# An attention layer's row maxima: which units use a difference, and where the fourth maximum stands in TensorE's queue

## The reference

```python
q = (hidden_states @ wq).reshape(B, S, H, D)      # B, S, H, D = 4, 1024, 16, 16
k = (hidden_states @ wk).reshape(B, S, Hkv, D)    # Hkv = 4
v = (hidden_states @ wv).reshape(B, S, Hkv, D)
...
scores = jnp.einsum('bqkgd,bskd->bkgqs', qg, k) * scale
attn = jax.nn.softmax(scores, axis=-1)
out = jnp.einsum('bkgqs,bskd->bqkgd', attn, v).reshape(B, S, E)
...
x = _layernorm(x + _L0_attn_ref(...), axis=-1)
x = _layernorm(x + _L0_ffn_ref(...), axis=-1)
```

## Time and profile before

| | us |
|---|---|
| median of 3 runs | 1069.21 |
| lowest, highest | 1068.98, 1076.9 |
| the profiled execution | 1073.24 |
| its span, first to last instruction | 1071.2 |

### The profile page before, as it was taken

The page is one execution under the profiler, slowest core; times in us unless marked ns, Lnnn a source line. Parts: engine busy times, 40 slices in busy tenths (PEclk is TensorE's granted clock), DMA queues, the critical chain, the costliest instruction groups (busy, mean ns, idle before and its releaser), DMA issues.

```text
span 1071.2 us, 16022 instructions
## 1 busy us (share of the span) xinstructions
PE 988.0 (92%) x5632; PEld 485.4 (45%) x5632; DVE 807.5 (75%) x1601; ACT 710.3 (66%) x908; POOL 237.4 (22%) x162
## 2 busy tenths in 40 slices
PE   7886999999999999999999999999998899999985
PEld 3443433333333333333333333333333778778774
DVE  2756688888788888888788888888862677777756
ACT  1224588888888888888888888888885433333332
POOL 9854563000000000000000000000000444444443
PEclk9885599999999999999999999999999999999997
DMA  5659532032132331322304213131110201111001
GB/s 164 222 172 187 127 103 64 26 75 78 32 65 57 69 63 44 71 55 50 78 22 79 73 39 64 52 72 42 29 49 12 61 0 41 40 40 40 20 20 40
DMA packets 48450, 70.65 MB, mean 66 GB/s; under 512 B 15152, under 2 KB 27184, under 8 KB 48368
## 3 DMA queue, kind: packets, MB, share of 16 engines
q1 hardware_dynamic: 47552, 66.45, 24.6%
q0 software_dynamic: 816, 3.15, 0.9%
HBM read 46.47 MB, written 16.25 MB: 59 GB/s over the span
## 4 chain that ended last, share of the span: by engine, by line
PE 59%; DVE 21%; issue 5%; POOL 4%; ACT 4%; POOLq 0%; DVEq 0%; ACTq 0%
PE ring_bank L948 25%; PE pv_bank L971 23%; DVE block_max L607 15%; PE pair_bank L1068 6%; POOL hid_l L528 2%; PE pv_bank L1077 2%; PE pair_bank L1021 1%; ACT probs L867 1%; DVE hid L758 1%; PE ring_bank L1077 1%; DVE x L675 1%; POOL rstd L513 1%; PE ring_bank L987 1%; ACT hid_h L883 1%; ACT silu L893 1%
## 5 line engine op out<-in xcount | busy, mean ns | idle before, releaser
L867 ACT ACTIVATE probs<-pair_bank 128x1024 f32<-128x1024 f32 x512 | 496.7, 1028 | 54.3 <-PE pair_bank L1021 54.3
L607 DVE TENSOR_REDUCE block_max<-ring_bank 128x1 f32<-128x512 f32 x660 | 421.8, 685 | 114.5 <-PE ring_bank L948 111.4
L948 PE MATMUL ring_bank<-k_max,q_sb 64*128 64x512 f32 x1024 | 365.1, 492 | 37.1 <-DVE block_max L607 9.8
L948 PEld LDWEIGHTS ring_bank<-k_max,q_sb 64*128 64x128 f32 x1024 | 148.0, 191 | 365.3 <-DVE block_max L607 224.3
L971 PE MATMUL pv_bank<-probs,v_sb 128*32 128x512 f32 x2048 | 274.5, 608 | 1.4 <-ACT probs L867 1.3
L1021 PE MATMUL pair_bank<-q_sb,k_sb 64*128 64x512 f32 x1024 | 230.9, 403 | 1.9 <-ACT probs L867 1.9
L838 ACT ACTIVATE above<-ring_bank 128x512 f32<-128x512 f32 x182 | 109.4, 603 | 73.7 <-PE ring_bank L948 70.7
L509 POOL TENSOR_TENSOR attn<-attn,inv_rows 128x1024 f32<-128x1024 f32 x8 | 19.5, 2434 | 590.3 <-DMA inv_rows<-inv_d 590.3
L1021 PEld LDWEIGHTS pair_bank<-q_sb,k_sb 64*128 64x128 f32 x1024 | 138.1, 186 | 23.6 <-ACT probs L867 15.5
L604 DVE CUSTOM_DVE_ANT_0 above<-ring_bank,above 128x512 f32<-128x512 f32 x182 | 123.8, 687 | 12.7 <-ACT above L838 11.3
L893 ACT ACTIVATE silu<-pair_bank,gate_s 128x512 f32<-128x512 f32 x64 | 44.0, 689 | 125.3 <-PE pair_bank L1068 125.3
(11 more groups left out here) (95 smaller groups left out, 883.5 us busy)
## 6 DMA issues: line engine op xcount, KB each, us to landing
q_sb<-q_parts SPq DMA_DIRECT2D x192, 64.0 KB, 2.3
k_max<-k_parts SPq DMA_DIRECT2D x96, 96.0 KB, 3.3
k_sb<-k_parts SPq DMA_DIRECT2D x96, 64.0 KB, 2.8
x_in<-xT SPq DMA_DIRECT2D x8, 512.0 KB, 5.0
q_parts<-high SPq DMA_DIRECT2D x16, 256.0 KB, 4.4
q_parts<-low SPq DMA_DIRECT2D x16, 256.0 KB, 4.4
attn<-pv_sb SPq DMA_DIRECT2D x128, 32.0 KB
inv_rows<-inv_d SPq DMA_DIRECT2D x64, 64.0 KB, 2.2
```

The costliest lines, as they stand in the source:

```text
L607: dve.reduce_max(block_max[half % 2][:, col:col + 1], bank[:], axis=AX.X).then_inc(ring_used, 1)
L867: act.activation(probs[t % 2][:, 2 * pr:2 * pr + 2, :], pair_bank[pr][:], ACT.Exp, scale=D ** -0.5).then_inc(probs_ready, 1)
L948: pe.matmul(bank[:], q_sb[k][rows, i, qt * P:(qt + 1) * P], k_max[k // QH][rows, kind * CH:(kind + 1) * CH], start=True, stop=True).then_i ...
```

## The change

`MIXED` becomes (0, 2, 4, 6): in every second unit one pair goes by the difference, four units of a half for five before. In those units maximum 3 stands ahead of the value matmuls; in the others the order stays: maxima 0, 1, 2, value matmuls, maximum 3. The order of the maxima among themselves, so the ring's order, is as before.

```diff
-MIXED = (0, 1, 3, 4, 6)
+MIXED = (0, 2, 4, 6)
...
                         scores(1)
                         maxima(2)
+                        if t in MIXED:
+                            maxima(3)
                         if not (first and k == 0 and t == 0):
                             pe.wait_ge(probs_ready, 2 * g)
                             if t:
                                 pv(g - 1, n, k, t - 1, first and k == 0)
                             else:
                                 pv(g - 1, n - 1, (k - 1) % HALVES, KT - 1, True)
-                        maxima(3)
+                        if t not in MIXED:
+                            maxima(3)
```

## The result

| | before | after |
|---|---|---|
| median, us | 1070.64 (4 runs) | 1012.36 (4 runs) |
| lowest, highest | 1068.98, 1076.9 | 1012.01, 1014.48 |
| span of the profiled execution | 1071.2 | 1012.7 |

The changed kernel takes 0.9456 of the time of the one before, with a 95% interval of 0.9437 to 0.9476. The forecast was 1011, in 1003 to 1040. The span shrank by 58.5 us. The changed kernel was run a second time beside the experiments: 1013.19, ratio 0.9458 (0.9438 to 0.9479).

The account below looks back on a forecast made before the run. Bound: a loop of waits between DVE's reads and the score maxima through a ring of three banks, not a full engine. 3 x 0.58 + 0.28 = 2.02 per half, x 30 = 60.6, less 3: 58 us; from 1069.21 to 1011, range 1003 to 1040.

Parts of the forecast that it names:

- The loop: Attention units: DVE's read of the last unit's maximum 3, maximum 2 and the value matmuls wait in turn, 2.70 us a unit.
- The even unit at 2.70, m3 for nothing: Units with a difference: maximum 3 starts beside maximum 2 at 1.28, costs nothing, and the unit still takes 2.70 us.
- The odd unit at 2.12, the pair at 4.82: Units without a difference: maximum 2 comes without a wait, 2.12 us; a pair takes 4.82 for 5.40, gain 0.58.
- m2 0.23 after m1: Sign that the prediction is right: in odd units maximum 2 starts 0.23 us after maximum 1.
- The pair t = 0, 1: First two units of a half, with the row maxima's transpose: 5.36 us for 5.64, gain 0.28 (0 to 0.38).
- The reciprocal: DVE instruction of 0.53 us after the split, 7 times: makes DVE's reads 0.4 us late, a loss of 3 us in all.
- Sum: Gain of 3 x 0.58 + 0.28 = 2.02 us per half, x 30 = 60.6, less 3: 58 us.
- ACT as the next bound: ScalarE is late next, with 0.03 to 0.1 us to spare; rival that it takes the loop's place: 1023 to 1047, chance 0.12.
- L948 would wait for DVE about half as long: Sign in the waits: weight loads of the score maxima, which waited 200.9 us for DVE, wait about half as long.
- 0 by themselves: Changed read counts: DVE's total rises 18 us, ACT's falls 18 us, both beside the loop, so no effect on the time.

## Why the prediction was right, step by step

**The loop.** Right. It was one of m3', DVE's read, m2 and the value matmuls, and the number of reads was not in it: with the new set alone the seven plain units of a half stay at 2.70.

**The even unit at 2.70, m3 for nothing.** Right: m2 and m3 start together at 1.28, the value matmuls at 1.70 or 1.71. The rule of the Trainium skill (TensorEngine Tiling (Array Packing), Key Properties), that a change of mode drains the array while tiles of one mode run in parallel, agrees in both parts: 0.43 from the start of m2 and m3 to the value matmuls, as before with m2 alone, where two matmuls of one mode are 0.23 apart.

**The odd unit at 2.12, the pair at 4.82.** Right to the hundredth (403.05 to 405.17, 400.35 to 405.17), but not by the steps that I gave. I had m0 start alone, m1 at 0.57 and m2 0.23 behind it. In the trace the unit's first two matmuls, m0 and one of s0, start together (403.05 and 403.06), m1 comes at 0.34 (403.39), and m2 is the one that starts alone, at 0.80, 0.46 behind m1. My sign "m2 0.23 after m1" thus failed. Four starts stand before the value matmuls either way (0, 0.34, 0.57, 0.80), so the sum kept its 0.80; that the wrong order didn't cost anything is luck.

**The pair t = 0, 1.** I had 5.36, it is 5.41. Two errors partly cancel: m1 follows the transpose after 0.20 and not 0.33, but m2 then waits for DVE's read of m0 and comes at 3.99 for my 4.04, and from a m2 behind a wait to the value matmuls it is 0.42 and not the 0.33 of one without. 0.05 x 30 = 1.5 us too much gain.

**The reciprocal.** I took 3 us off, and it costs nothing: in all seven places the unit behind it still has its m2 1.28 to 1.29 after the start. DVE's row for one of them (the pair begins at 385.29, the next one at 390.70):

```profile
389.65 0.53 DVE L649 RECIPROCAL inv_sums<-sums 128x64 f32<-128x64 f32 x1
390.11 2.49 DVE L607 TENSOR_REDUCE block_max<-ring_bank 128x1 f32<-128x512 f32 x4
```

I had let the reciprocal start where the record of the split ends (4.53 after the pair's start), m1's read where that of the reciprocal ends, and the next m3' where that of m2's read ends: 0.4 late. In the trace each starts before the record ahead of it ends: the reciprocal at 4.36, m1's read at 4.82, 0.46 behind it, and the read of the next m3' at 5.96, where 5.94 is its time without a reciprocal. 3 us too little gain.

**Sum.** 3 x 0.58 + 0.23 = 1.97, x 30 = 59, and the span shrank by 58.5. The forecast's 58 was that close also by luck: the last two errors have opposite signs.

**ACT as the next bound.** The direction was right, the size wrong: its room is 0.15 per pair, where I gave 0.03 to 0.1. I had let the difference start when the record of the exponential before it ends; ACT takes the next instruction some 0.1 earlier (an exponential of 1.03 is followed after 0.90 to 0.92).

**A marker read wrongly.** I wrote that L948 would wait for DVE about half as long. In the waits of the kernel after, from 200 to 740 us:

```profile
PEld ring_bank L948 <- DVE block_max L607: 132.4, 211, 0.8
PEld ring_bank L948 <- DVE block_max L604: 88.0, 105, 0.8
```

Together that is 220, over 200.9 in the earlier trace rows. But these rows mix two kinds of idle time. In front of a maximum that comes behind the value matmuls PEld idles 0.84, the time of these matmuls, whoever is named: that is 107 of the 320 waits before and 204 of the 316 after. The others are in the main the waits of m2, which are the loop: 213 of some 0.52 before, 111 us in all, and 112 of 0.30 to 0.52 after, 49 us in all. So the wait of the loop did fall to under half; the row as I named it couldn't show it. The row for the other direction shows it too: DVE waited 98.3 us for L948 and now 24.7.

**What the prediction hadn't seen.** I had written of the new set's counts "0 by themselves". By itself the set costs 1.1%, some 12 us, through t = 1, where it changes who reads m0. It didn't spoil the sum, because I had worked the pair out anew with DVE reading m0. But it means that the order, given the new set, is worth some 70 us (the ratios 1.0108 and 0.9456, of about 1070), and the set takes part of it back.

## What to carry to other kernels

In a loop through a ring of buffers, ask for each write whose read it waits for and what stands behind it in its own queue. Moving one write ahead of a long step is free where the engine waits at that place anyway and the bank's reader is early; done in every iteration, the wait only moves to the write that was moved. Something that takes a place in the ring once in a while shifts which buffer everyone behind it waits for: its best place is where the buffers before and after it have early readers.

## What the runs showed of the hardware

A DVE copy from SBUF to SBUF of 128 x 128 fp32 takes 0.20 to 0.22 us, and took 0.9 to 2.8 us in the 11 places where GpSimd was at work, each ending 0.08 to 0.09 us after GpSimd's instruction; a DVE reduction over the same tile took 0.26 to 0.28 us in all 120 places, 12 of them beside GpSimd. By the Trainium skill (SBUF — State Buffer, Who interferes with whom), a copy in a two-port mode and GpSimd hold a shared pair of ports in turn, each for a whole instruction, and a reduction on trn2 never contends; these runs agree, though they don't show the copy's mode. For this kernel that is a warning: DVE has 0.3 us to spare per pair, and the form of an instruction put there decides whether it is free.
